# Where the tensor engine loads and unpacks its tile table word in a mixture-of-experts kernel

## What is computed

```python
x = x + xattn(layernorm(x), ctx)                     # 32 x 112 tokens, context of 375 rows
xf = layernorm(x).reshape(-1, 256)
scores = sigmoid(xf @ gate_w.T + lb_bias)            # 8 experts
topw, topi = top_k(scores, 2)
for e in range(8):
    y = (silu(xf @ gate[e].T) * (xf @ up[e].T)) @ down[e].T      # 256 -> 128 -> 256
    out = out + where(selected(e), y * mean_weight(e), 0)
out = out + shared_mlp(xf)                           # 256 -> 256 -> 256
```

## Time and profile before

| | us |
|---|---|
| median of three runs | 467.94 |
| profiled execution | 463.88 |
| its span (first to last instruction) | 462.12 |
| tile stage, from its first table load to its last down product | 303.6 to 411.9 |
| of it, from step 5 on | 317.85 to 411.9 |

### The profile page before, as it was taken

The page is one execution under the profiler, slowest core; times in us unless marked ns, Lnnn a source line. Parts: engine busy times, 40 slices in busy tenths (PEclk is TensorE's granted clock), DMA queues, the critical chain, the costliest instruction groups (busy, mean ns, idle before and its releaser), DMA issues.

```text
span 462.1 us, 9868 instructions
## 1 busy us (share of the span) xinstructions
PE 384.2 (83%) x2628; PEld 337.6 (73%) x2628; DVE 281.3 (61%) x1079; ACT 225.6 (49%) x528; POOL 243.6 (53%) x288
## 2 busy tenths in 40 slices
PE   0858999998989899898979696569999999979940
PEld 0836777886868777677869595458999999969940
DVE  0343666666777666677697848525554554515996
ACT  0234577665556646545646534025656666645110
POOL 1254777544386666668786752712665666662000
PEclk9988999999999999999989978659999999999995
DMA  8975334211122222221411220234555555425999
GB/s 196 229 204 141 118 102 139 72 50 40 51 86 63 80 83 65 82 66 41 132 41 42 71 68 24 81 92 123 166 158 155 164 162 159 130 78 113 258 264 319
DMA packets 40197, 54.44 MB, mean 118 GB/s; under 512 B 5678, under 2 KB 31025, under 8 KB 40018
## 3 DMA queue, kind: packets, MB, share of 16 engines
q1 hardware_dynamic: 32514, 38.32, 31.6%
q0 software_dynamic: 6144, 14.75, 9.3%
q10 hardware_dynamic: 1488, 0.75, 0.6%
HBM read 34.34 MB, written 20.51 MB: 119 GB/s over the span
## 4 chain that ended last, share of the span: by engine, by line
PE 53%; DVE 21%; issue 12%; POOL 5%; DMA 3%; ACT 2%; SPq 1%; ACTq 1%; DVEq 1%; POOLq 0%
PE x2t_ps L1377 9%; PE q_ps L1258 6%; PE ct_ps L1285 6%; PE s_ps L1238 4%; PE pt_ps L1397 4%; DVE x_sb L749 3%; PE s_ps L1397 3%; POOL rstd L557 3%; PE o_ps L1296 3%; DVE stats L613 3%; PE x2t_ps L1247 3%; PE x2t_ps L1200 2%; POOL token_rows L540 2%; PE pt_ps L1276 2%; PE o_ps L1355 2%
## 5 line engine op out<-in xcount | busy, mean ns | idle before, releaser
L588 POOL DMA_INDIRECT expert_rows<-tile_out,row_to x64 | 62.8, 982 | 54.0 <-ACT tile_out L1133 43.6
L540 POOL DMA_INDIRECT token_rows<-send,send_rows x64 | 64.9, 1014 | 29.5 <-issue 16.5
L563 POOL TENSOR_SCALAR ctx_norm<-ctx_raw,rstd,minus_mean_rstd 125x192 f32<-125x192 f32 x96 | 46.9, 498 | 48.8 <-issue 38.5
L557 POOL TENSOR_TENSOR rstd<-var_eps,minus_half 128x5 f32<-128x5 f32 x39 | 46.6, 1195 | 35.8 <-DVE var_eps L637 35.4
L1238 PE MATMUL s_ps<-ctx_norm_t,q_t 97*112 97x375 f32 x128 | 45.9, 480 | 2.2 <-ACT probs L1052 1.2
L1030 ACT ACTIVATE ctx_norm_t<-x2t_ps 97x750 f32<-97x750 f32 x32 | 25.5, 796 | 39.7 <-PE x2t_ps L1247 39.7
L1285 PE MATMUL ct_ps<-probs_t,ctx_norm 125*97 125x112 f32 x384 | 43.2, 263 | 0.0
L1285 PEld LDWEIGHTS ct_ps<-probs_t,ctx_norm 125*97 125x97 f32 x384 | 40.2, 168 | 0.0
L1377 PE MATMUL x2t_ps<-gate_up_hi,tile_t_hi 128*128 x128 | 39.4, 308 | 0.0
L1258 PE MATMUL q_ps<-x_norm_t,a_sb 128*97 128x224 f32 x128 | 30.0, 381 | 9.5 <-DVE logits_sb L757 9.5
L1377 PE MATMUL x2t_ps<-gate_up_lo,tile_t_hi 128*128 x128 | 36.6, 286 | 0.0
(11 more groups left out here) (239 smaller groups left out, 1096.2 us busy)
## 6 DMA issues: line engine op xcount, KB each, us to landing
ctx_raw<-in_ctx_in SPq DMA_DIRECT2D x32, 281.2 KB
tile<-token_rows SPq DMA_DIRECT2D x64, 129.0 KB
back<-expert_rows SPq DMA_DIRECT2D x16, 448.0 KB, 11.0
out<-x_sb SPq DMA_DIRECT2D x8, 448.0 KB, 7.9
x_sb<-in_x SPq DMA_DIRECT2D x1, 3136.0 KB, 27.2
stage<-in_gate_up_t SPq DMA_DIRECT2D x8, 320.0 KB, 3.2
token_rows<-send SPq DMA_DIRECT2D x8, 129.0 KB, 4.2
token_rows<-send,send_rows POOLq DMA_INDIRECT x64, 2.7
```

Of the source, the lines that this page charges most:

```text
L540: nc.gpsimd.indirect_dma_start(token_rows, bass.IndirectOffsetOnAxis(ap=SLOT[:, b, k:k + 1], axis=0), SEND[0:T, b % RING, :], None, bounds ...
L557: nc.gpsimd.tensor_tensor(RS[:, j, :], VE[:, j, :], HALF[:, :], ALU.pow).then_inc(rstd_ready, 1)
L563: nc.gpsimd.tensor_scalar(X2N[:, (i + 3) % 4, t, 0:DC], RAW[:, (i + 3) % 4, t, :], RS[0:KP, j, t:t + 1], NM[0:KP, j, t:t + 1], ALU.mult, A ...
L588: nc.gpsimd.indirect_dma_start(expert_rows, bass.IndirectOffsetOnAxis(ap=DEST[:, p % 4, k:k + 1], axis=0), YO[p % OUTS][:, k, :], None, bo ...
```

## The change

The load of the next word moves from behind the gate/up product to behind its fourth matmul. The fields are no longer taken out where they are used: a new function `units` takes two of them into registers of their own, the gate/up fields behind the tile transposes and the down fields behind the eighth gate/up matmul. Steps without a gate/up product do both directly ahead of the down product.

```diff
+            def word(i):
+                if not (pair(i - 1) or pair(i - 4)):
+                    return None
+                return nc.values_load(TAB[0:1, i:i + 1], engines=(pe.engine,), min_val=0,
...
+            def units(table, first, size):
+                last = (UNITS if first == 0 else E) - 1
+                at = []
+                for k in range(2):
+                    r = pe.alloc_register()
+                    pe.reg_mov(r, offset(table, first + k, size))
+                    at.append(pe.snap(r, min_val=0, max_val=last * size))
+                return at
+
...
                     last.then_inc(tt_done, 1)
+                if pair(i - 1):
+                    at_gate_up = units(table, 0, GATE_UP)
                 if pair(i - 3):
...
+                following = None
                 if pair(i - 1):
...
                     for k in range(2):
-                        at = offset(table, k, GATE_UP)
                         n = 0
...
-                                                        w[:, bass.ds(at + kt * 2 * TILE, 2 * TILE)],
+                                                        w[:, bass.ds(at_gate_up[k] + kt * 2 * TILE, 2 * TILE)],
                                                         start=n == 0, stop=n == 3 * DT - 1)
                                 n += 1
+                                if (k, n) == (0, 4):
+                                    following = word(i + 1)
+                                if (k, n) == (1, 2) and pair(i - 4):
+                                    at_down = units(table, 2, D)
                     last.then_inc(tg_done, 1)
-                following = None
-                if pair(i) or pair(i - 3):
-                    following = nc.values_load(TAB[0:1, i + 1:i + 2], engines=(pe.engine,), min_val=0,
...
+                else:
+                    following = word(i + 1)
+                    if pair(i - 4):
+                        at_down = units(table, 2, D)
...
                     for k in range(2):
-                        at = offset(table, 2 + k, D)
...
-                                                    v[:, p % 2, k * TILE:(k + 1) * TILE], w[:, bass.ds(at, D)],
-                                                    start=n == 0, stop=n == 2)
+                                                    v[:, p % 2, k * TILE:(k + 1) * TILE],
+                                                    w[:, bass.ds(at_down[k], D)], start=n == 0, stop=n == 2)
```

More of the change, by code:

```diff
@@ L1347, in offset @@
                                           skip_runtime_bounds_check_because="the table is made of units")
+            def word(i):
+                if not (pair(i - 1) or pair(i - 4)):
+                    return None
+                return nc.values_load(TAB[0:1, i:i + 1], engines=(pe.engine,), min_val=0,
+                                      max_val=(GATE_UP << 4 * FIELD) - 1,
+                                      skip_runtime_bounds_check_because="it has four fields")
+            def units(table, first, size):
[6 more added lines that the diff above has]
+                return at
             def tile_step(i, table):
@@ L1377, in tile_step @@
                                 last = nc.tensor.matmul(g_ps[:, p % 2, k * 256:(k + 1) * 256], v[:, p % 2, cols],
-                                                        w[:, bass.ds(at + kt * 2 * TILE, 2 * TILE)],
+                                                        w[:, bass.ds(at_gate_up[k] + kt * 2 * TILE, 2 * TILE)],
                                                         start=n == 0, stop=n == 3 * DT - 1)
                                 n += 1
+                                if (k, n) == (0, 4):
+                                    following = word(i + 1)
+                                if (k, n) == (1, 2) and pair(i - 4):
+                                    at_down = units(table, 2, D)
                     last.then_inc(tg_done, 1)
-                following = None
-                if pair(i) or pair(i - 3):
-                    following = nc.values_load(TAB[0:1, i + 1:i + 2], engines=(pe.engine,), min_val=0,
-                                               max_val=(GATE_UP << 4 * FIELD) - 1,
-                                               skip_runtime_bounds_check_because="it has four fields")
+                else:
+                    following = word(i + 1)
+                    if pair(i - 4):
+                        at_down = units(table, 2, D)
                 if pair(i - 4):
```

## The result

| | kernel before | changed kernel |
|---|---|---|
| median, us | 466.79 | 470.81 |
| lowest and highest, us | 463.86 to 468.73 | 469.52 to 472.94 |
| runs | 12 | 12 |
| profiled execution, us (span) | 463.88 (462.12) | 470.78 (469.0) |

A forecast was written before the change was run, and what follows sets the result against it. The prediction took PE's sequencer to bound the tile stage: load 0 plus register work +5.9 us on 467.94 gave 473.8 us, 1.3% slower, with a range of 469.5 to 478.0.

The forecast's parts named there:

- The sequencer is the bound: Tile stage: PE's in-order instruction list sets the 3.18 us step, while the matmul array has slack at 2.82 us.
- The load, cost 0 with a range of -3.5 to +4.2: Table load moved into the gate/up product: cost 0 at the median of 415 ns, bounds -3.5 and +4.2 us.
- The register work, +5.9: Register operations on PE in the tile stage: 59 more on the path at 0.10 us each, +5.9 us.
- the difference in kind I take at nothing: Register work of a step: swapping 2 ALU operations fewer for 4 fused ones more was priced at nothing.
- The sum: Whole kernel: +5.9 us on the median of 467.94 gives 473.8 us, 1.3% slower.
- What lies behind the stage: After the tile stage: nothing has slack against a later stage, so the 5.9 us arrives at the end in full.
- The gap closes: Rival, down product: the array is the bound and the load hides behind queued matmuls, 457.9 us; chance 0.06.
- The added operations cost little: Rival, register work: added operations vanish in a stop of the list, 0.02 us each, 469.1 us; chance 0.06.
- The load gets shorter: Rival, table load: all loads take 298 ns in the new place, +2.4 us, 470.3 us; chance 0.06.
- The clock falls: Rival, tile stage: more array idling lowers the clock, 1.6 us more per low step, three give 478.6; chance 0.04.
- What would show it: Signs in the tile stage: step 3.38 us, waits of 0.2 to 0.5 behind the fourth matmul, 0.2 to 0.4 behind the eighth.

The follow-up runs named there:

- units alone: Changed kernel with its load put back behind the twelfth gate/up matmul: 474.31 us, on a chip where the kernel before took 488.52.
- a word for two steps: units kept, with a table word holding two pairs' experts and loaded only every second step: 458.53 us, ratio 0.9833 to the kernel before.
- four more ALU: Kernel before with one more ALU operation on each of the four fields: 477.96 us, on a chip where the kernel before took 488.52.
- before, again: Kernel before, unchanged, profiled a second time on another chip: 466.2 us.
- load alone: Kernel before with only the load moved behind the fourth gate/up matmul: ratio 0.9946 on the 488.52 us chip; again on another chip, 463.73 us, ratio 0.9888.
- load behind eighth: Kernel before with the load moved behind the eighth gate/up matmul: 462.67 us in one run, beside 466.17 for the kernel before.
- units kept: load alone, with each tile's gate/up offset also kept in a register until its down product: 462.33 us, ratio 0.9933 to the kernel before.

## Why the prediction was right, and which terms were off

**The sequencer is the bound.** Right. The step follows its list in five kernels (3.10, 3.17, 3.32, 3.34, 3.46) and single steps stop at 2.79 where the list is shorter than the array's work; the place of the load, compared at equal length (3.32 for 3.34), moves it by 0.02 us.

**The load, cost 0 with a range of -3.5 to +4.2.** The value chosen was the wrong one. The argument for the median, that the array reads weights at both places, fell: the length is 301 ns in its new place, and also at the old place once the units are taken out early (units alone). The term measured is 30 x (0.301 - 0.417) = **-3.5 us**, the range's lower end and the rival to which 0.06 was given. The earlier trace rows had held a hint, since a short and a long load stand in one trace; what set them apart was not looked for.

**The register work, +5.9.** The count was right, 672, and so was 0.10 us for an ALU operation (0.099 measured). Wrong was "the difference in kind I take at nothing". The list without the load grew from 2.764 to 3.32 - 0.301 = 3.02 us, 0.26 a step instead of 0.20. With 0.099 for each of the two ALU operations taken out, the four fused ones cost (0.26 + 0.20) / 4 = 0.114 us each. The bar had said so: 54 ns at the median in L1361 against 37 in the earlier trace rows. The term measured is 28 x 0.26 = **+7.3 us**, +0.3 for the three short steps at 0.1 each.

The Trainium skill states a floor of about 20 cycles an instruction (Runtime: NRT & Kernel Launch, Instruction fetch mechanics). The prediction had an estimate of 1.0 us from it and said that the trace does not agree. A floor is not contradicted by what lies above it: the 0.10 us of every run here are about six times the prediction's 0.017, and say only that the floor is no price for a register operation.

**The sum.** -3.5 + 7.6 = +4.1 us, measured 4.0. Two errors of -3.5 and +1.7 partly cancelled, so the forecast held better than its terms, and that much of it was luck.

**What lies behind the stage**, 1:1: the 4 us of the stage are the 4.0 of the medians.

**The rivals.** *The gap closes*: the gap before the down product did close, yet the time did not fall, since the sequencer opened others. It wins only with a shorter list, and there it did, at -8.5 us with a word for two steps. *The added operations cost little*: refuted by four more ALU, 0.099 each. *The load gets shorter*: it did, as above; its +2.4 for the time fell short of the +4.0 by the register work. *The clock falls*: 1.00 from 320 to 410.

**What would show it.** The step, 3.38, was 3.32; behind the eighth matmul 0.2 to 0.4 was 0.36 by the lateness of the weight load (0.29 idle); behind the fourth 0.2 to 0.5 was only 0.13, with a load of 0.30 there for 0.42. "Loads whose median is not near 415" was named as what would show the forecast wrong, and it did, for that term.

## What to carry to other kernels

Where the array idles in short pieces and no semaphore is late, count what its sequencer does in a step before moving anything: a stall that is moved comes back elsewhere, and only what shortens the list pays: an operation taken out, or a load that becomes shorter. Here a register operation cost 0.10 us, nearly a 128x256 matmul at 0.12, so keeping an offset for its second use, and loading a word for two steps, gained 8.5 us where moving the load alone gained 3.0. Price each kind of operation for itself, and ask of a duration that varies twofold in one trace what it varies with before its median goes into a sum.

## What was not expected of the hardware

**The length of a table load.** It is 296 to 314 ns, or longer by up to 0.4 us. Ordered by how many weight loads that stand ahead of it in the list had not yet started when the load began, the means are:

| kernel | 1 to 2 | 3 | 4 | 5 and more |
|---|---|---|---|---|
| before | | 383 (2) | 396 (10) | 435 (15) |
| before, again | | 303 (2) | 413 (12) | 437 (13) |
| changed | 301 (27) | | | |
| load alone, again | 304 (2) | 306 (10) | 321 (15) | |
| load behind eighth | 304 (10) | 302 (17) | | |
| units alone | 309 (27) | | | |
| four more ALU | 301 (7) | 302 (20) | | |
| units kept | 426 (2) | 298 (1) | 479 (13) | 390 (11) |
| a word for two steps | 335 (4) | | 451 (1) | 300 (8) |

(ns, in brackets the number of loads.) With up to three queued all but five loads are under 330 ns, and with four or more in the kernel before most are long, as if the queue made the length. The other rows say that it does not do so alone: load alone has four queued for 15 loads and 11 of them are 312 ns or less, a word for two steps has six or seven queued for eight loads and all are 296 to 303, and units kept has one of 553 with two queued. What makes a load long is open. The Trainium skill gives a floor of about 600 ns for a `tensor_load` (DMA: Bandwidth & Descriptors, Latency and other measured facts); of this one, a word from the table in SBUF, the trace shows half of that, 296 ns.

**Pauses of the sequencers.** On one chip the kernel before took 488.5 us instead of the 466 to 468 of the others, and two kernels with short lists showed 16 and 18 us of stretches in which the sequencers of all five engines start nothing, each 0.4 to 0.7 us long, in groups about 7.5 us apart. Kernels with 0.15 to 0.28 us more in each step had at most one. In the kernel before, the changed kernel and load alone on the other chips there is none; what looks like one in load alone there, 0.8 us of PE's sequencer, is a wait for a tile. The changed kernel was not run on that chip itself, but units alone, with the same operations, was 3.1% faster than before there: by this the sign of such a change can depend on the chip. The cause of the pauses is open.
